# Spreading softmax reciprocals over the partitions: a DMA round trip in place of a TensorE transpose

## The reference

```
scores = jnp.einsum('ehd,ehd->eh', q[src], k[dst])
smax = jax.ops.segment_max(scores, src, num_segments=N)
ex = jnp.exp(scores - smax[src])
denom = jax.ops.segment_sum(ex, src, num_segments=N)
attn = ex / denom[src]
out = jax.ops.segment_sum(attn[:, :, None] * v[dst], src, num_segments=N)
return out.reshape(N, D) @ wo + bo
```

## Time and profile before

| what | before |
|---|---|
| median of 3 runs | 1912.09 us (1910.96 to 1913.0) |
| the profiled execution's own time | 1910.58 us |
| its span | 1908.8 us |
| TensorE busy (matmul rows) | 1845.7 us, 97% |
| VectorE busy | 1113.5 us, 58% |
| ScalarE busy | 700.8 us, 37% |
| 16 DMA engines, share of the span | 12.2% |

### The profile page before, as it was taken

The page is one execution under the profiler, slowest core; times in us unless marked ns, Lnnn a source line. Parts: engine busy times, 40 slices in busy tenths (PEclk is TensorE's granted clock), DMA queues, the critical chain, the costliest instruction groups (busy, mean ns, idle before and its releaser), DMA issues.

```text
span 1908.8 us, 31400 instructions
## 1 busy us (share of the span) xinstructions
PE 1845.7 (97%) x11066; PEld 1526.2 (80%) x11067; DVE 1113.5 (58%) x2389; ACT 700.8 (37%) x924; POOL 339.2 (18%) x395
## 2 busy tenths in 40 slices
PE   4999999999999999989999999899999999999998
PEld 4888655587888888878888888788888887888887
DVE  6998835634555577335554773355548744555475
ACT  2102230113565441225654422155653312556532
POOL 3000441300000244000001640000016300000173
PEclk8999999999999999999999999999999999999999
DMA  3001301121010101110101011200010112000011
GB/s 119 0 0 55 134 1 56 49 77 42 29 42 1 39 23 51 58 62 15 56 1 38 23 51 37 84 15 31 27 38 23 31 56 82 15 29 28 23 66 66
DMA packets 38731, 79.64 MB, mean 42 GB/s; under 512 B 10856, under 2 KB 10856, under 8 KB 38592
## 3 DMA queue, kind: packets, MB, share of 16 engines
q1 hardware_dynamic: 38592, 77.82, 12.2%
HBM read 66.14 MB, written 11.67 MB: 41 GB/s over the span
## 4 chain that ended last, share of the span: by engine, by line
PE 65%; issue 31%; DVE 1%; POOL 1%; ACT 1%; POOLq 0%; ACTq 0%; DVEq 0%; PEldq 0%
PE ps L1237 39%; PE ps L1171 7%; PE ps L1262 5%; PE ps L1295 4%; PE ps L1227 4%; PE ps L1288 2%; PE ps L1196 2%; PE ps L1301 2%; PE ps L1346 2%; POOL film L524 0%; ACT counts L637 0%; PE ps L1350 0%; POOL kh L577 0%; DVE masked_s L953 0%; PE ps L1158 0%
## 5 line engine op out<-in xcount | busy, mean ns | idle before, releaser
L1262 PE MATMUL ps<-pT,v 128*128 128x256 f32 (+1 forms) x1600 | 370.5, 379 | 4.2 <-ACT pT L750 4.1
L689 ACT ACTIVATE s<-masked_s,small 128x1280 f32 (+1 forms) x156 | 213.3, 1367 | 339.6 <-DVE small L956 339.6
L1237 PE MATMUL ps<-yT,w 128*128 128x512 f32 (+1 forms) x1728 | 335.5, 355 | 0.0
L1262 PEld LDWEIGHTS ps<-pT,v 128*128 128x128 f32 x1600 | 292.1, 190 | 42.9 <-ACT pT L750 9.1
L1237 PE MATMUL ps<-kh,q_parts 128*128 128x512 f32 (+3 forms) x1440 | 318.0, 365 | 5.4 <-DVE v L1038 3.4
L1237 PEld LDWEIGHTS ps<-yT,w 128*128 128x128 f32 x1728 | 281.5, 190 | 49.3
L1237 PEld LDWEIGHTS ps<-kh,q_parts 128*128 128x128 f32 (+1 forms) x1440 | 249.0, 189 | 52.4 <-issue 4.8
L1237 PE MATMUL ps<-w,kh 128*128 128x512 f32 (+1 forms) x960 | 235.4, 396 | 2.5 <-POOL kh L577 2.5
L750 ACT COPY pT<-ps 128x1408 f32<-128x1408 f32 (+1 forms) x160 | 206.8, 1292 | 3.8 <-PE ps L1350 3.8
L1237 PEld LDWEIGHTS ps<-w,kh 128*128 128x128 f32 (+1 forms) x960 | 174.3, 186 | 41.3 <-POOL kh L577 2.8
L953 DVE CUSTOM_DVE_ANT_0 masked_s<-ps,mask 128x1280 f32<-128x1280 f32 x96 | 143.2, 1491 | 92.0 <-PE ps L1237 92.0
(11 more groups left out here) (164 smaller groups left out, 1960.9 us busy)
## 6 DMA issues: line engine op xcount, KB each, us to landing
mask<-mask_dram SPq DMA_DIRECT2D x24, 640.0 KB, 4.1
w_raw<-in_L_gnn_m_w_dram SPq DMA_DIRECT2D x8, 1024.0 KB, 5.5
mask_y<-mask_dram SPq DMA_DIRECT2D x12, 640.0 KB, 4.1
mask_dram<-mask_out SPq DMA_DIRECT2D x10, 640.0 KB, 2.9
w_l<-in_L_gnn_W_dram SPq DMA_DIRECT2D x2, 2048.0 KB, 10.0
w_raw<-in_L_gnn_wq_dram SPq DMA_DIRECT2D x4, 1024.0 KB, 5.7
w_raw<-in_L_gnn_wk_dram SPq DMA_DIRECT2D x4, 1024.0 KB, 5.3
w_raw<-in_L_gnn_wv_dram SPq DMA_DIRECT2D x4, 1024.0 KB, 5.4
```

Source lines behind the costliest of these rows:

```text
L689: nc.scalar.activation(to, masked_of(u), ACT.Exp, bias=small[0:R, u % 2, 1:2], accum_out=small[0:R, u % 2, 2:3]).then_inc(exp_done, 1)
L1237: mine = mm(to, left(a), right(b), start=first and n == 0, stop=final and n == 2)
L1262: mine = mm(ps[:, 6 + gh % 2, 0:wd], v[:, t, h * P:(h + 1) * P], pT[:, gh % 2, t, 0:wd], start=(t == 0), stop=(t == NT - 1))
```

## The change

The tile `rep`, its VectorE instruction and its transpose go away, on all 160 units. The reciprocals of a pair go to a small tile `rec` (128 x 1 for each unit). SP writes each of the two columns to a DRAM buffer, waits for both to land, and loads the up to 256 numbers back, broadcast to all 128 partitions, into the same slot `pT[..., NT, ...]`. ScalarE copies ten tiles in place of eleven, and `head_output` waits for the load rather than for the copy. SP's loads of masks 5 to 9 are placed between these transfers.

```diff
+    rec_dram = nc.dram_tensor("rec_dram", (2, 2 * P), F32, kind="Internal").ap()
...
+            def spread_reciprocals(gh, i):
+
+                g = gh // H
+                sp.wait_ge(rec_ready, i * U + 2 * gh + 2)
+                sizes = [rows(2 * g), rows(2 * g + 1)]
+                for k, R in enumerate(sizes):
+                    sp.dma_start(rec_dram[gh % 2, k * P:k * P + R].rearrange("(p o) -> p o", o=1),
+                                 rec[0:R, gh % 2, k:k + 1]).then_inc(rec_saved, 16)
+                sp.wait_ge(rec_saved, (i * GH + gh + 1) * 32)
+                if gh >= 2:
+                    sp.wait_ge(head_out, i * GH + gh - 1)
+                wd = sum(sizes)
+                sp.dma_start(pT[:, gh % 2, NT, 0:wd], rec_dram[gh % 2:gh % 2 + 1, 0:wd].broadcast_to([P, wd])).then_inc(rep_in, 16)
...
-                for t in range(2, NT):
-                    if t >= 5:
+                for t in range(2, 5):
+                    load_mask(t)
+                for gh in range(GH):
+                    spread_reciprocals(gh, i)
+                    for t in range(5, NT):
                         old = max(n for n in range(t) if MASK_PLACE[n] == MASK_PLACE[t])
-                        sp.wait_ge(masked, i * U + UNITS.index((old // 2, H - 1, old % 2)) + 1)
-                    load_mask(t)
+                        last_use = UNITS.index((old // 2, H - 1, old % 2))
+                        if last_use // 2 == gh:
+                            sp.wait_ge(masked, i * U + last_use + 1)
+                            load_mask(t)
...
-                    nc.scalar.copy(pT[:, gh % 2, :, k * P:k * P + R], turn[:, :, 0:R]).then_inc(pT_out, 1)
+                    nc.scalar.copy(pT[:, gh % 2, 0:NT, k * P:k * P + R], turn[:, :, 0:R]).then_inc(pT_out, 1)
...
-                dve.wait_ge(pT_out, i * U + 2 * gh + 2)
+                dve.wait_ge(rep_in, (i * GH + gh + 1) * 16)
...
-                    dve.wait_ge(den_s, (i * U + u) * 2 + 1)
-                    nc.vector.reciprocal(small[0:R, u % 2, 3:4], small[0:R, u % 2, 2:3]).then_inc(den_s, 1)
-                    dve.wait_ge(den_s, (i * U + u) * 2 + 2)
-                    if u >= 1:
-                        dve.wait_ge(turned, i * U + u)
-                    nc.vector.tensor_scalar(rep[0:R, :], ident[0:R, :], 0.0, small[0:R, u % 2, 3:4], ALU.mult,
-                                            ALU.add).then_inc(rep_ready, 1)
+                    dve.wait_ge(den_s, i * U + u + 1)
+                    nc.vector.reciprocal(rec[0:R, u // 2 % 2, k:k + 1], small[0:R, u % 2, 2:3]).then_inc(rec_ready, 1)
...
-                    pe.wait_ge(rep_ready, i * U + u + 1)
...
-                    nc.tensor.transpose(turn[:, NT * P:NT * P + R], rep[0:R, :], ident[0:R, 0:R]).then_inc(turned, 1)
+                    mine.then_inc(turned, 1)
```

More of the change, by code:

```diff
@@ L237, in gnn_kernel @@
         small = sb("small", [P, 2, 4])
+        rec = sb("rec", [P, 2, 2])
         eps1 = sb("eps1", [P, 1])
@@ L346, in gnn_kernel @@
         scored, masked, negm_s, exp_done = sem("scored"), sem("masked"), sem("neg_max"), sem("exp_done")
-        den_s, rep_ready = sem("denominator"), sem("reciprocal_spread")
+        den_s, rec_ready, rec_saved, rep_in = sem("denominator"), sem("reciprocal"), sem("reciprocal_saved"), sem("reciprocal_spread")
         turned, pT_out, summed, head_out = sem("turned"), sem("weights_out"), sem("summed"), sem("head_out")
@@ L748, in attention @@
                         act.wait_ge(head_out, i * GH + gh - 1)
-                    turn = ps_flat[:, 3 * BANK:3 * BANK + (NT + 1) * P].rearrange("p (t r) -> p t r", r=P)
-                    nc.scalar.copy(pT[:, gh % 2, :, k * P:k * P + R], turn[:, :, 0:R]).then_inc(pT_out, 1)
+                    turn = ps_flat[:, 3 * BANK:3 * BANK + NT * P].rearrange("p (t r) -> p t r", r=P)
+                    nc.scalar.copy(pT[:, gh % 2, 0:NT, k * P:k * P + R], turn[:, :, 0:R]).then_inc(pT_out, 1)
                     if 0 <= u - U // 2 < KD:
@@ L1345, in attention @@
                         if u:
-                            nc.tensor.transpose(turn[:, t * P:t * P + R].bitcast(F32R),
-                                                s_of(u)[:, t * P:(t + 1) * P].bitcast(F32R), ident_r[0:R, 0:R])
-                        else:
-                            nc.tensor.transpose(turn[:, t * P:t * P + R], s_of(u)[:, t * P:(t + 1) * P], ident[0:R, 0:R])
-                    nc.tensor.transpose(turn[:, NT * P:NT * P + R], rep[0:R, :], ident[0:R, 0:R]).then_inc(turned, 1)
+                            mine = nc.tensor.transpose(turn[:, t * P:t * P + R].bitcast(F32R),
+                                                       s_of(u)[:, t * P:(t + 1) * P].bitcast(F32R), ident_r[0:R, 0:R])
+                        else:
+                            mine = nc.tensor.transpose(turn[:, t * P:t * P + R], s_of(u)[:, t * P:(t + 1) * P], ident[0:R, 0:R])
+                    mine.then_inc(turned, 1)
             products(qkv0, zero_now, 0)
```

## The result

The changed kernel takes 1965.76 us (median of 4 runs, 1962.78 to 1968.04); the kernel before took 1912.32 us beside it. The ratio is 1.0281, 95% interval 1.0269 to 1.0293: 53 us slower, where 18 us faster were forecast.

What follows compares the result with a forecast made beforehand. Bound: TensorE's own 9.70 us a pair and, just above, a chain through ScalarE's copy of 9.90 us. Gains of 15.6 + 2.3 = 17.9 us from 1910.58, plus 1.5 for the median, gave 1894 us; range 1888.5 to 1903.

Steps and rivals of the forecast that it cites:

- the round trip through DRAM (added): Attention, 80 pairs with three DMAs each: home 6.9 us after the reciprocal, under 9.5 us of cover, so zero cost.
- Rival A: Round trip comes home late and VectorE's `head_output` waits; loss begins beyond 15.1 us; 1921 to 1967 us; chance 0.08.
- The idling before the weighing and the chain that sets it: Mid-attention: TensorE idles 0.20 us a pair awaiting ScalarE's copy, on a chain of 9.90 us a pair; the idling stays.
- the transpose at 0.10 us: TensorE in attention: removing the eleventh transpose saves 0.10 us each (0.085 to 0.145), not its 300 ns in flight.
- the copy at 0.105 us: ScalarE's copy out of PSUM, once a pair on the chain: 128 columns fewer save 0.105 us (0 to 0.12).
- The cover of 13.3 and 9.5 us: Time from a pair's second reciprocal to its `head_output`: 13.3 us in mid-attention, 9.5 us at a block's end.
- SP's later masks and weights: SP's queue: loads of masks 5 to 9 and `M1`'s weights issue later but before they are wanted; zero cost.
- B: Attention pairs: only one of the two limits moves, a pair gains 0.10 us and idling grows; 1902.6 us; chance 0.09.
- C: TensorE in attention: the removed transpose costs its full 300 ns, so 33 us are gained; 1879 us; chance 0.03.
- D: Attention: nothing comes of it, transposes already hide in TensorE's queue; only 2.3 us at block starts; 1910 us; chance 0.04.
- The sum of the attention: Four blocks: 76 intervals between pairs, each 0.205 us shorter from transpose and copy, give 15.6 us.
- The start of the blocks: Masks no longer wait for VectorE's removed instruction, and the first copy is shorter: 2.3 us over four blocks.

Runs made afterwards that it cites:

- the second experiment: Changed kernel with both stores and the wait for them, but the load takes 1 KB of the input x: 1920.03 us, ratio 1.0056.
- a free round trip: Changed kernel with stored numbers 512 bytes apart in DRAM and the load taking 1 KB of the input x: 1895.99 us, ratio 0.9919.
- both full kernels: Changed kernel with the buffer in SBUF in place of DRAM, 1899.91 us; changed kernel with one store of 8 bytes a partition, 1898.85 us.

## Why the prediction was wrong

**The step that failed** is the term "the round trip through DRAM (added)", put at zero. It put the way home at 6.9 us from the landing of a 640 KB store (2.9 us) and of a 256 KB load (2.8 us). It was 14.3 us at the median and up to 23.6, over the cover of 13 us in 62 of 80 pairs. Of its parts the stores were mis-sized most: 8.3 us after the issue of the second in place of 2.9. The load, 4.4 in place of 2.8 us, was off by less, but the second experiment (1920 us) shows that most of the 53 us would not be there if the load did not read the row just written. The prediction had a small transfer of 7.7 us before it, put it down to the crowd at the kernel's start, and used it for the upper bound alone. The spaced places show that it is the closeness of 4-byte writes that makes the stores slow, and the buffer in SBUF that this belongs to DRAM.

**Rival A** was the mechanism that came true, at a chance of 0.08. That +53 us is near its figure for 17 us (+55) is luck: by its rule a way home of 14.3 us costs nothing, since the loss begins at 15.1 us. Three things were missing in it:

- *It gave all trips one size.* They went from 11.4 to 23.6 us, and 27 of 80 were over 15.1 us. What these lie over it adds up to 65 us. Rival A counts half of that, which holds when all pairs are late alike. A single late pair would delay everything behind it by the whole of its excess, and the measured loss, 70 us against a free round trip (1896 us), is near the whole. With the close stores and the load of other data 11 pairs are over by 20 us in all, and the loss is 24 us. (An estimate from the ways home of each pair; no run tests it by itself, and for the kernel with one store of 4 bytes, where nearly all are late alike, the whole is far too much: 137 us, for 87 us over 1896.)
- *It asked whether a trip is shorter than its cover, not whether the queue is free for the next.* SP waits in order, so for each pair it is taken for landing and issues, 9.0 us at the median from the first store to the load, out of 9.70. A turn longer than that makes the next start late (by up to 4.0 us). A mask load ahead of the stores does it in the timeline above: 11.1 us from 495.59, and the stores for the reciprocal of 505.07 went out at 507.16. With one store of 4 bytes, where SP's turn took 10.6 us, nearly every trip was late although all but one were shorter than 13.0 us. In the changed kernel 11 of the 27 pairs over 15.1 us are late only by SP's turn, the trip from the first store on being shorter; the other 16 trips are too long in themselves. With the load of other data all 11 trips over 15.1 us are too long in themselves.
- *A late load meets the next pair's stores.* The load issued at 515.60 was home at 525.74, after 10.1 us, with the next stores issued right behind it (516.03). The view of line L455 of the changed kernel gives:

```profile
DMA to landing us min/median/max: 3.0/4.4/10.2
```

In the kernel with one 4-byte store, where SP lets the load land before it issues the next store, the longest load took 5.0 us; with stores 512 bytes apart 5.0 us; with the close stores and a load of other data 9.7 us. That the next stores hold the load up fits all of these, but was not tried by itself. It can't be all: of the changed kernel's 67 loads with the next stores at most 3 us behind them 12 took over 6 us and 55 did not; of the other 13 none did.

**What was right.** The idling before the weighing and the chain that sets it, though it was to stay at 0.20 us and is 0.15 us in the stretch above; the transpose at 0.10 us (measured 0.09) against its 300 ns in flight; the copy at 0.105 us (0.11); the pair at 9.69 us (9.70 to 9.72). The cover of 13.3 and 9.5 us: with a way home of 8.9 us or less (both full kernels) no `head_output` waited. SP's later masks and weights cost nothing there; in the changed kernel the mask loads lengthened the landing of the stores behind them from 8.1 to 10.5 us, which the prediction's zero for SP's queue did not have. With stores 512 bytes apart they did not (1.5 us with and without). Rivals B, C and D did not come.

**What was a little off.** The sum of the attention: 76 intervals at 0.205 us were to give 15.6 us; from the first to the last `head_output` the four blocks gave 732.3 - 719.7 = 12.6 us with stores 512 bytes apart. The first interval of a block fell by 0.05 us, the last four by 0.13 us on average, those between by 0.18 to 0.20 us, not 0.205. The start of the blocks, from the first exponential to the first `head_output`, gave 96.4 - 93.2 = 3.2 us where 2.3 were expected, 2.2 us of it in the third block alone. This part varies: the other kernels without waits gave 0.6 to 3.5 us, so it neither bears out the 2.3 us nor speaks against them. Less the 2 us by which that program reaches its first attention later, 12.6 + 3.2 comes near the 13.7 us between the spans, 1908.8 and 1895.1.

## What to carry to other kernels

A wait that is moved from a compute engine to a DMA has two limits: the longest trips, not only the median one, must be shorter than the work that covers them, and what the issuing queue does for one turn, waits included, must be shorter than the period at which turns come. Before a small transfer is priced by a large one, look at where its pieces go: one number from each of 128 partitions into a compact DRAM row is slower (8.3 us) than 640 KB into long rows (2.9 us). Here two plain remedies turned 53 us of loss into 13 us of gain: widening each partition's piece from 4 to 8 bytes with one store in place of two, or staging the row in SBUF.

## What the runs showed of the hardware that was not expected

- 4-byte writes to DRAM in places 4 bytes apart landed 7.0 to 7.5 us after their issue, whether 128 or 256 of them, and 8.3 us where the load reads what they wrote; 8 bytes apart 3.1 us; from 64 bytes on 1.5 us. All 64-byte pieces that were slow held 16 writes. Whether the piece that counts is 32 or 64 bytes, and whether writes of different engines or any writes collide in it, stays open. Places 16 and 32 bytes apart were not tried.
- Loading 1 KB from one SBUF row to all 128 partitions took 6.3 us, and from a DRAM row that nothing had just written 3.0 us. From the row just written it took 4.1 us (one store of 8 bytes) and 4.4 us (the changed kernel). The Trainium skill, "DMA: Bandwidth & Descriptors", Anatomy of one DMA, has about 2 us fixed for a transfer, most of it the receipt. It says so of DMAs that GpSimd issues; here SP issues them. The landings of 1.5 us from the second issue on with spaced places agree with it in size; those of compact rows do not, and the way home of some 4 us that the prediction took from it was 14.3 us.
- TensorE's clock. After the wait of 7.46 us on VectorE, in which TensorE stood idle for 4.20 us, the windows show a granted clock of 0.50, its lower level of 1.2 GHz, and then 0.87 as a mean over the next 10 us (columns: stretch, length, busy us of PE, PEld, DVE, ACT and POOL, granted clock, DMA share, GB/s):

```profile
500.00:520.00 20.00, 20.00 (x120) 17.43 (x119) 8.96 (x23) 11.45 (x17) 0.00 (x0) 1.00 0.22 15
520.00:526.00 6.00, 3.92 (x25) 3.29 (x24) 0.23 (x1) 0.66 (x1) 0.00 (x0) 0.98 0.00 0
526.00:530.00 4.00, 1.88 (x5) 1.49 (x5) 2.18 (x7) 1.60 (x3) 0.00 (x0) 0.50 0.42 37
530.00:540.00 10.00, 10.00 (x56) 8.81 (x55) 4.62 (x12) 4.95 (x6) 0.00 (x0) 0.87 0.02 0
```

  The scores that start then take 3.37 us to the weighing and the weighing 2.53 us to the transposes, where 1.87 and 2.07 us are usual in this trace:

```profile
528.12 3.57 PE L1253 MATMUL ps<-kh,q_parts 128*128 128x512 f32 x9 [4.20 <-DVE small L974]
531.49 2.88 PE L1278 MATMUL ps<-pT,v 128*128 128x256 f32 x10
534.02 1.15 PE L1361 MATMUL ps<-ident,s 128*128 128x128 f32 x10
```

  This stall thus cost about 2 us more than its own length. Over the whole execution the mean was 0.978, against 0.994 before.
- Programs that differ only in the attention reach it at either about 447.2 or 449.1 to 450.7 us. The cause was not found.
